# Attention's PSUM banks: four for the scores of the maxima and two for those of the exponentials, instead of three and three

## The reference

```
q, k, v = proj(Wq, bq), proj(Wk, bk), proj(Wv, bv)        # per head [T, 8]
scores  = where(k_pos > q_pos, -inf, q @ k.T * 8 ** -0.5)  # causal
p       = softmax(scores - max(scores))
out     = (p @ v) @ Wo.T + bo
```

## Time and profile before

| | |
|---|---|
| median of 3 runs | 1939.92 us (1939.84 to 1942.79) |
| the profiled execution's own time | 1940.62 us |
| its span, first to last instruction | 1938.6 us |
| granted TensorE clock, mean of the span | 0.907 |
| PE busy | 1586.9 us (82%) |
| DVE busy | 1378.0 us (71%) |
| ACT busy | 970.3 us (50%) |
| POOL busy | 649.8 us (34%) |
| first and last reduction for a maximum (L562) | 77.9 and 931.7 us |
| first and last exponential (L611) | 101.9 and 957.3 us |

### The profile page before, as it was taken

The page is one execution under the profiler, slowest core; times in us unless marked ns, Lnnn a source line. Parts: engine busy times, 40 slices in busy tenths (PEclk is TensorE's granted clock), DMA queues, the critical chain, the costliest instruction groups (busy, mean ns, idle before and its releaser), DMA issues. The chain is left out here.

```text
span 1938.6 us, 42434 instructions
## 1 busy us (share of the span) xinstructions
PE 1586.9 (82%) x13842; PEld 1031.8 (53%) x13842; DVE 1378.0 (71%) x2515; ACT 970.3 (50%) x2357; POOL 649.8 (34%) x494
## 2 busy tenths in 40 slices
PE   5599989998999998999862924699999999976193
PEld 3233333333333333333452824699999999976083
DVE  6788888898888888889260331478998988974222
ACT  4167777777776777777630211134444444432020
POOL 5400000000000000000025431396988888832632
PEclk9689999999999999999965967899999999986597
DMA  3200000000000000000082120111111111105323
GB/s 106 95 18 19 13 18 19 19 18 13 17 19 20 19 15 15 19 19 10 2 268 66 51 57 17 37 35 45 52 43 54 44 43 54 43 11 174 134 67 106
DMA packets 88425, 91.93 MB, mean 47 GB/s; under 512 B 11316, under 2 KB 72876, under 8 KB 87988
## 3 DMA queue, kind: packets, MB, share of 16 engines
q1 hardware_dynamic: 84148, 81.17, 13.9%
q0 software_dynamic: 4096, 8.46, 1.2%
HBM read 40.91 MB, written 25.56 MB: 34 GB/s over the span
## 5 line engine op out<-in xcount | busy, mean ns | idle before, releaser
L562 DVE TENSOR_REDUCE chunk_max<-ps_max 128x1 f32<-128x512 f32 (+3 forms) x1280 | 704.2, 604 | 104.0 <-PE ps_max L667 57.3
L611 ACT ACTIVATE probs<-ps_s 128x512 f32<-128x512 f32 (+3 forms) x1280 | 612.7, 536 | 216.2 <-PE ps_s L659 107.4
L1424 POOL TENSOR_TENSOR lane_products<-L,q 128x1024 f32<-128x1024 f32 x176 | 411.0, 2373 | 154.7 <-DMA L<-ident_rows 104.8
L640 PE MATMUL ps_s<-Qs,Ks 50*128 50x512 bf16 (+3 forms) x1280 | 369.2, 355 | 37.5 <-DVE chunk_max L562 22.1
L650 PE MATMUL ps_max<-Ks,Qs 48*128 48x512 bf16 (+3 forms) x1280 | 378.3, 361 | 13.2 <-POOL a_ident L504 10.6
L712 PE MATMUL ps_o<-probs,Vp 128*32 128x512 f32 (+3 forms) x2560 | 344.7, 564 | 5.2 <-ACT O_sb L594 4.8
L640 PEld LDWEIGHTS ps_s<-Qs,Ks 50*128 50x128 bf16 x1280 | 98.7, 94 | 369.9 <-DVE chunk_max L562 315.1
L519 POOL TENSOR_TENSOR A_b<-A_newton,b_tile 128x128 f32<-128x128 f32 x32 | 14.6, 457 | 812.6 <-ACT A_newton L614 812.6
L1473 DVE TENSOR_TENSOR weighted<-exp_scores,psV_s 128x2048 f32<-128x2048 f32 x88 | 197.0, 2280 | 0.0
L1566 PE MATMUL psZT<-ident,weighted 128*128 128x128 f32 x1408 | 167.2, 274 | 1.8 <-DVE weighted L1473 1.8
L1566 PEld LDWEIGHTS psZT<-ident,weighted 128*128 128x128 f32 x1408 | 157.9, 142 | 2.0 <-DVE weighted L1473 2.0
(11 more groups left out here) (223 smaller groups left out, 2242.8 us busy)
## 6 DMA issues: line engine op xcount, KB each, us to landing
m_w<-in_L_ffn_w_dram SPq DMA_DIRECT2D x32, 512.0 KB, 7.1
Qs<-q_parts SPq DMA_DIRECT2D x192, 32.0 KB
Ks<-k_parts SPq DMA_DIRECT2D x192, 32.0 KB
dispatched<-m_blank SPq DMA_DIRECT2D x2, 2080.0 KB
m_blank<-dispatched SPq DMA_DIRECT2D x16, 260.0 KB, 2.7
routed<-m_blank SPq DMA_DIRECT2D x2, 2048.0 KB
L<-q SPq DMA_DIRECT2D x8, 448.0 KB
q_parts<-parts SPq DMA_DIRECT2D x8, 384.0 KB, 2.5
```

What stands on the lines that cost most here:

```text
L562: nc.vector.tensor_reduce(out, scores[:, 0:w], axis=AX.X, op=ALU.max).then_inc(max_reduced, 1)
L611: nc.scalar.activation(dst, ps_s[(k + r) % R][:, q0:], ACT.Exp, scale=SCALE).then_inc(exp_done, 1)
L640: last = nc.tensor.matmul(ps_s[(k + r) % R][:, q0:], K[r][rows, kt * P:(kt + 1) * P], Q[r][rows, g * QW + q0:(g + 1) * QW], start=True, st ...
L1424: return nc.gpsimd.tensor_tensor(out[:, l].rearrange("p (j m) d -> p j m d", m=LA), c.L[ch][:, :, l * LW:(l + 1) * LW].unsqueeze(2).broadc ...
```

## The change

`MB` banks hold the scores of the maxima and `SB` those of the exponentials, 4 and 2. A step's bank is now its number modulo 4 or modulo 2, without the head's number, which works as 40 steps are a multiple of both. The two waits in front of a pair are made to fit: maximum k-4 and exponential k-2. Nothing else is changed; the operations and their order on each engine are the same.

```diff
@@ attend @@
+    MB, SB = 4, 2
...
+    assert NS % MB == 0 and NS % SB == 0
...
-        ps_max = [ps(f"ps_max{u}") for u in range(R)]
-        ps_s = [ps(f"ps_s{u}") for u in range(R)]
+        ps_max = [ps(f"ps_max{u}") for u in range(MB)]
+        ps_s = [ps(f"ps_s{u}") for u in range(SB)]
...
-                    scores, out = ps_max[(k + r1) % R], chunk_max[r1][:, i, ck:ck + 1]
+                    scores, out = ps_max[k % MB], chunk_max[r1][:, i, ck:ck + 1]
...
-                        nc.scalar.activation(dst, ps_s[(k + r) % R][:, q0:], ACT.Exp, scale=SCALE).then_inc(exp_done, 1)
+                        nc.scalar.activation(dst, ps_s[k % SB][:, q0:], ACT.Exp, scale=SCALE).then_inc(exp_done, 1)
...
-                last = nc.tensor.matmul(ps_s[(k + r) % R][:, q0:], K[r][rows, kt * P:(kt + 1) * P],
+                last = nc.tensor.matmul(ps_s[k % SB][:, q0:], K[r][rows, kt * P:(kt + 1) * P],
...
-                last = nc.tensor.matmul(ps_max[(k + r) % R][:, 0:w], Q[r][rows, i * P:(i + 1) * P],
+                last = nc.tensor.matmul(ps_max[k % MB][:, 0:w], Q[r][rows, i * P:(i + 1) * P],
...
-                last = nc.tensor.matmul(ps_s[(k + r) % R][:, q0:q0 + HALF], c.causal[rows, 0, half, :], c.ident_b[rows, rows],
+                last = nc.tensor.matmul(ps_s[k % SB][:, q0:q0 + HALF], c.causal[rows, 0, half, :], c.ident_b[rows, rows],
...
-                last = nc.tensor.matmul(ps_max[(k + r) % R][:, k0:k0 + HALF], c.causal[rows, 1, half, :],
+                last = nc.tensor.matmul(ps_max[k % MB][:, k0:k0 + HALF], c.causal[rows, 1, half, :],
...
-                    wait(pe, exp_done, s * NS + (k - 2))
+                    wait(pe, exp_done, s * NS + (k - SB + 1))
...
-                    pe.wait_ge(max_reduced, (s + 1) * NS + (AHEAD + k - 2))
+                    pe.wait_ge(max_reduced, (s + 1) * NS + (AHEAD + k - MB + 1))
```

## The result

The changed kernel takes 2065.12 us (median of 4 runs, 2056.82 to 2071.82) against 1939.88 us (4 runs, 1938.26 to 1942.79): ratio 1.0646, interval [1.0626, 1.0667]. It is slower, as forecast, but by 125 us and not by 91, and outside the range that was given (1996 to 2052). Its runs also spread over 15 us, those of before over 4.5. The profiled execution is the longest, 2071.82 us, with a span of 2069.8.

What follows compares the result with a forecast made beforehand. No single engine was full; the order of TensorE's queue with its bank waits decided. Terms of 2.92 us a head made 93 over 32 heads, less some 2: 1940.6 + 91 = 2031.6, forecast 2031 us, range 1996 to 2052.

Steps and rivals of the forecast that it cites:

- each plain round: Steps 27-30: third pair waits for the first exponential (+1.08), fourth for the second (+1.57); +0.36 us a round.
- VectorE's extra bank: Looser wait on maxima: its gain was already in the sum; a possible second gain of 8 us was taken as nothing.
- combine rounds: Steps 11-14 and 23-26: 1.0 us of combine matmuls already puts the fourth pair past +1.57; no loss.
- the rounds with ScalarE's copies: Steps 3-6 and 15-18: fourth pair waits for the exponential behind a copy; +0.82 and +0.50 us, the least sure terms.
- 39, 0-2: Round with short exponentials: a transpose waiting for VectorE covers nearly all of the delay; +0.07 us, an estimate.
- Release: At each wait on an exponential, TensorE issues the pair 0.05 us after the exponential's end, as read in the last head.
- The bound set on this term (0.07): Release may be 0.07 instead of 0.05 us, over 8 waits a head and 32 heads: +5 us.
- Off that go some 2 us: At loop restarts and in the half-clock first head, TensorE's own streaming covers the exponentials: 93 us becomes +91.
- The rival of the falling clock: Longer TensorE gaps lower its clock, about +1.3 us in one round in ten: +42 us, 2073 or more; chance 0.06.
- the maxima did not set the pace: Rival: maxima set the pace and the third exponential bank was spare; 22 us faster, 1918; chance 0.04.
- the copies moved with their exponentials: Rival: rounds with copies lose nothing, as ScalarE reaches them at another point; 1.60 us a head, 1990; chance 0.10.
- ScalarE's idle time did not take up the shallower queue: Rival of no change: ScalarE's idle time absorbs the shallower queue of exponentials; chance 0.03.

Runs made afterwards that it cites:

- experiment 6: The changed kernel with three banks for the maxima and two for the exponentials, one PSUM bank unused: 2074.76 us.
- experiment 5: The changed kernel with ScalarE's two copies of O one exponential later, behind 4 and 16: 2034.21 us.
- experiment 7: The changed kernel mirrored, two banks for the maxima and four for the exponentials: 2097.19 us.
- experiment 1: The changed kernel with the two waits in front of a pair in the other order, maximum first, exponential last: 2057.06 us.
- experiment 2: The changed kernel with the wait on the maxima written twice: 2102.5 us.
- experiment 8: The kernel before with its two waits in the other order, exponential last: 1951.56 us, ratio 1.0062.
- experiment 3: The changed kernel with all 32 heads written out, no loop in attention: 2031.23 us.
- experiment 4: The kernel before with all 32 heads written out, no loop in attention: 1934.61 us, ratio 0.9957.
- experiment 12: The kernel with three maxima and two exponential banks, plus two idle matmuls in seven rounds a head, written to the unused bank: 2062.85 us, against 2074.76 without.
- experiment 10: The changed kernel with eight of ten batches of P·V products a head cut into halves, the second half issued later: 2082.59 us.

## Why the prediction was off

The mechanism, the sign and the places were right. The two-bank queue of the exponentials makes each plain round wait for its first and second exponential in the middle; VectorE's extra bank gives a head nothing (experiment 6); combine rounds kept their 2.95 us; the rounds with ScalarE's copies lost most, and moving the copies gave 0.78 us back (experiment 5); the mirror image came out at the 4.5 us a head worked out for it (experiment 7). Round by round, one head of each kernel, from the starts of the pairs (us):

| steps | before | changed | longer by | forecast | experiment 1 |
|---|---|---|---|---|---|
| 3-6 (copies) | 2.28 | 3.15 | 0.87 | 0.82 | 3.08 |
| 7-10 | 2.51 | 2.91 | 0.40 | 0.32 | 2.84 |
| 11-14 (combine) | 2.95 | 2.95 | 0 | 0 | 2.95 |
| 15-18 (copy) | 2.85 | 3.45 | 0.60 | 0.50 | 3.37 |
| 19-22 | 2.50 | 2.91 | 0.41 | 0.33 | 2.84 |
| 23-26 (combine) | 2.95 | 2.95 | 0 | 0 | 2.95 |
| 27-30 (plain) | 2.53 | 2.96 | 0.43 | 0.36 | 2.88 |
| 31-34 | 2.71 | 2.96 | 0.25 | 0.16 | 2.88 |
| 35-38 | 2.48 | 2.91 | 0.43 | 0.36 | 2.84 |
| 39, 0-2 | 2.39 | 2.62 | 0.23 | 0.07 | 2.54 |
| a head | 26.15 | 29.77 | 3.62 | 2.92 | 29.17 |

Every round that was priced came out 0.05 to 0.16 us longer than its price, and turning the two waits takes 0.07 to 0.08 off each of them. The size failed in two steps.

*Release.* "So TensorE issues 0.05 us after the exponential's end" was read in the last head. There only one wait stands in front of a pair. Everywhere else two do, and the change moves the blocking from the second to the first. Then the satisfied one behind it still has to be gone through: 0.13 us instead of 0.06, shown by turning the order and by doubling the wait (experiments 1, 2, 8), and once more by the written-out kernels, whose order is turned (3, 4). The bound set on this term (0.07) came from a blocking wait that stands last, so it was no bound for one that stands first. It makes 0.61 of the 0.70 us a head that were missing, about 20 us over attention in a head-by-head sum. That the label on the waits named the maximum nearly hid this.

*The clock.* "Off that go some 2 us" for the restarts had the wrong sign. The heads with restarts took 12 us more than before, 1 of it longer pauses, and the ends some 9 more. The rival of the falling clock was held at 0.06 because the last head of the kernel before kept its clock; but TensorE's longest wait in that head is 0.26 us, and in the changed kernel's 0.71, so it could not vouch for the change. (The stretch read for it, 900 to 950 us, also begins 31 us before that head.) The rival was right in kind: the changed kernel is at the lower level for 75 us instead of 19. Its price was right too: in the last head of experiment 6 a plain round takes 4.18 us at the lower clock, against 2.88 at full clock in experiment 12, 1.3 more. Where it expected the loss, in one round in ten all through attention, there was none. The page of the Trainium skill that spoke for it ("TensorE: Matmul & The Clock Gate", "A second HAM failure mode: psum-queue depth-cycling") agrees with the last heads alone, where experiments 3 and 6 lost the clock and experiment 12, with the gaps filled, kept it. In the heads before that, experiment 3 has waits of up to 0.71 us in every head and keeps its clock at 1.00. Why the lower clock lasts longer behind a restart since the change stays open: 51 us in all against 17 in the profiled executions, behind nearly the same pauses. From the measured rows the sum is 112 + 12 - 2 + 9 = 131 for the profiled execution. The median, 125, is lower, as the other three runs have a higher mean clock.

The other rivals fell as argued: the maxima did not set the pace, the copies moved with their exponentials, and ScalarE's idle time did not take up the shallower queue. The range was too narrow since it took the clock as a case by itself, instead of a term that every outcome has a share of.

## What to carry to other kernels

A bank taken from a queue is paid at the point where the producer comes back from other work: lay out one round by hand, and count from the first item after that work. Put the wait that will block last in front of the instruction, and trust an idle label only when moving the named event moves the wait. When a producer waits more often, add a term of its own for its clock, and look for it behind every long pause and where part of its stream is missing. When an edit is meant to change one thing (here, a loop written out), look in the trace whether the waits still stand in the order of the source.

## What the runs showed of the hardware

- A satisfied wait behind a blocking one costs TensorE 0.07 to 0.10 us. The gaps behind an exponential are 0.06, 0.13 and 0.23 us with none, one and two satisfied waits; behind a maximum they are 0.06 to 0.07 with none and 0.14 (looped) or 0.16 (written out) with one.
- Writing out the loop turned the order of two waits on TensorE's queue against the source (experiments 3 and 4). It made a head 0.55 us shorter where exponentials block and 0.37 us longer where maxima do.
- Two idle matmuls of 256 columns in seven rounds of a head made the kernel 12 us faster. The last head, 13.5 us shorter, kept its clock; the intervals with restarts got 3 us longer.
- The lower clock behind a pause of 2.8 to 3.6 us lasted from 3 to 24 us, and once, in experiment 7, 37 us. Behind the longer pauses of experiments 10 and 12 (4.3 to 4.8 us) it lasted 7 to 14. So the pause alone does not set it, and what does was not found.
- In the last head of the written-out changed kernel the clock fell with no wait of TensorE over 0.71 us. In the 30 heads before, with waits as long, it did not.
